# Attention on one core: where TensorE and VectorE load the bin numbers of a batch's tiles

## The reference, cut to what matters

```python
h = jnp.maximum(_layernorm(x, axis=-1), 0.0)
h = (h @ W.T).reshape(N, H, OUT)
a_src = (h * att_src).sum(-1)
a_dst = (h * att_dst).sum(-1)
alpha = jax.nn.leaky_relu(a_src[src] + a_dst[dst], 0.2)
amax = jax.ops.segment_max(alpha, dst, num_segments=N)
ex = jnp.exp(alpha - amax[dst])
denom = jax.ops.segment_sum(ex, dst, num_segments=N)
w = ex / denom[dst]
msg = h[src] * w[:, :, None]
out = jax.ops.segment_sum(msg, dst, num_segments=N)
x = x + out.reshape(N, H * OUT) + bias
```

## Time and profile before

| | |
|---|---|
| median of 3 runs | 5701.16 us |
| lowest and highest | 5682.81 and 5708.14 us |
| the profiled execution | 5682.86 us, of it span 5681.1 us |
| PE busy over the span | 90% |
| DVE | 69% |
| ACT | 52% |
| POOL | 68% |

### The profile page before, as it was taken

The page is one execution under the profiler, slowest core; times in us unless marked ns, Lnnn a source line. Parts: engine busy times, 40 slices in busy tenths (PEclk is TensorE's granted clock), DMA queues, the critical chain, the costliest instruction groups (busy, mean ns, idle before and its releaser), DMA issues.

```text
span 5681.1 us, 160364 instructions
## 1 busy us (share of the span) xinstructions
PE 5111.3 (90%) x34188; PEld 4074.0 (72%) x34189; DVE 3923.1 (69%) x14222; ACT 2971.1 (52%) x8485; POOL 3871.0 (68%) x3713
## 2 busy tenths in 40 slices
PE   4888888888888886999999999999997999999999
PEld 3777777777777774677666666666665888887788
DVE  6777877878778776555455555555455888888887
ACT  3566666666666653333333333332223777777776
POOL 4777777777777774677777777777776555555553
PEclk7889889889889987999999999999998999999999
DMA  4522222222222234999888988888886999999997
GB/s 109 165 54 54 54 54 54 54 54 54 54 54 54 54 105 139 278 275 270 262 263 258 266 262 260 262 264 259 262 257 186 224 221 222 222 221 217 217 222 193
DMA packets 860128, 995.58 MB, mean 175 GB/s; under 512 B 307993, under 2 KB 663225, under 8 KB 859776
## 3 DMA queue, kind: packets, MB, share of 16 engines
q1 hardware_dynamic: 662496, 610.19, 39.9%
q0 software_dynamic: 190592, 379.87, 24.6%
q10 hardware_dynamic: 6816, 3.38, 0.2%
HBM read 728.41 MB, written 264.62 MB: 175 GB/s over the span
## 4 chain that ended last, share of the span: by engine, by line
PE 59%; DMA 9%; issue 9%; DVE 9%; POOL 8%; DVEq 3%; ACT 3%; POOLq 0%; ACTq 0%; SPq 0%
PE bank L1703 12%; PE bank L1536 12%; PE bank L1626 8%; PE bank L1628 7%; PE bank L1693 7%; DMA xr<-arena 6%; POOL xr L547 5%; PE bank L1457 3%; POOL arena L499 2%; DVE arena L945 2%; DVEq L251 2%; DVE arena L1048 2%; PE bank L1616 1%; DMA arena<-xr 1%; DVE arena L1028 1%
## 5 line engine op out<-in xcount | busy, mean ns | idle before, releaser
L499 POOL DMA_INDIRECT arena<-h_tab,arena x1612 | 1557.1, 966 | 543.0 <-issue 420.7
L547 POOL DMA_INDIRECT xr<-arena x1612 | 1568.5, 973 | 511.7 <-issue 352.6
L1536 PE MATMUL bank<-arena 128*128 128x136 f32 x6448 | 1311.0, 332 | 78.3 <-DVE arena L1048 11.0
L719 ACT ACTIVATE arena<-bank 128x256 f32<-128x256 f32 x1612 | 591.3, 384 | 1389.6 <-PE bank L1628 932.0
L1626 PE MATMUL bank<-arena 128*128 128x256 f32 x3224 | 1023.4, 400 | 91.8 <-DVE arena L1244 45.1
L1536 PEld LDWEIGHTS bank<-arena 128*128 128x128 f32 x6448 | 980.9, 214 | 162.6 <-DVE arena L1048 67.0
L561 POOL DMA_INDIRECT arena<-p_tab,arena x428 | 671.3, 1569 | 622.3 <-DMA arena<-p_tab,arena 498.4
L626 ACT ACTIVATE arena<-bank 128x256 bf16<-128x256 bf16 x1612 | 614.7, 381 | 792.8 <-PE bank L1457 708.6
L1628 PE MATMUL bank<-arena 128*128 128x256 f32 x3224 | 971.3, 383 | 0.0
L1703 PE MATMUL bank<-arena 128*128 128x257 f32 x3424 | 901.5, 386 | 6.3 <-issue 2.6
L1048 DVE TENSOR_TENSOR arena<-arena,bank 128x272 f32 x1612 | 693.6, 430 | 212.7 <-PE bank L1536 186.0
(11 more groups left out here) (260 smaller groups left out, 6595.3 us busy)
## 6 DMA issues: line engine op xcount, KB each, us to landing
arena<-xr SPq DMA_DIRECT2D x428, 520.0 KB
arena<-q_tab SPq DMA_DIRECT2D x1612, 128.0 KB
arena<-in_edge_attr SPq DMA_DIRECT2D x61, 832.0 KB
arena<-rel_tab SPq DMA_DIRECT2D x124, 224.0 KB
arena<-h_tab,arena POOLq DMA_INDIRECT x1612
xr<-arena POOLq DMA_INDIRECT x1612
arena<-rel_tab SPq DMA_DIRECT2D x124, 192.0 KB
xr<-arena SPq DMA_DIRECT2D x26, 520.0 KB
```

Of the source, the lines that this page charges most:

```text
L499: pool.indirect_dma_start(G[:, q, t, :], None, h_tab, bass.IndirectOffsetOnAxis(ap=idx[:, q, t:t + 1], axis=0)).then_inc(sem(f"gath{q}"), 16)
L547: pool.indirect_dma_start(xr, bass.IndirectOffsetOnAxis(ap=pos[:, q, t:t + 1], axis=0), Rb[:, t, :], None).then_inc(sem(f"scat{m}"), 16)
L1536: last = pe.matmul(PSB[3 + t % 2][:, k * H * MW:(k + 1) * H * MW], OH[:, (t + 2 * q) % 4, k * P:(k + 1) * P], flat(msg[:, t, :, :]), start ...
```

## The change

TensorE and VectorE no longer load 26 bin numbers at the head of a batch. VectorE loads four at t=1, four at each of t=6, 10, 14, 18 and 22, ahead of that step's `add_up`, and two behind the last step. TensorE loads four at each of t=2, 6, 10, 14, 18 and 22, between that step's `turn` and `expand`, and two behind the last step. That makes 7 loads for each engine and batch, and the same 26 integers. In the last two batches TensorE has no load before and none after. The two batches of TensorE that stand ahead of the first one (0 and 1) keep their load of 26.

```diff
-        def bins(engine, b, count):
+        def bins(engine, b, first, count):
 
             return nc.values_load_multi_w_load_instructions(
-                bin_row[0:1, bass.ds(b * RB, count)], engines=[engine], min_val=0, max_val=NT - 1,
+                bin_row[0:1, bass.ds(b * RB + first, count)], engines=[engine], min_val=0, max_val=NT - 1,
...
-                a = flat(acc[:, bass.ds(regs[t], 2), :])
+                a = flat(acc[:, bass.ds(regs[t % 4], 2), :])
...
-                regs = bins(ENG.DVE, b, BT)
...
                     if t == 1:
+                        regs = bins(ENG.DVE, b, 0, 4)
                         dve.wait_ge(sem("r_step"), 4 * b + 4)
...
+                    if t >= 6 and t % 4 == 2:
+                        regs = bins(ENG.DVE, b, t - 2, min(4, BT - (t - 2)))
                     if t >= 2:
                         add_up(b, t - 2, regs)
...
+                regs = bins(ENG.DVE, b, BT - 2, 2)
                 add_up(b, BT - 2, regs)
                 add_up(b, BT - 1, regs)
...
             def batch(b, q, ahead2=True, ahead1=True, first=False, table=""):
-                if ahead2:
-                    regs = bins(ENG.PE, b + 2, BT)
...
                     if ahead2:
                         turn(b + 2, q, t)
+                        if t % 4 == 2:
+                            regs = bins(ENG.PE, b + 2, t - 2, min(4, BT - (t - 2)))
                         if t >= 2:
                             expand(b + 2, q, t - 2, regs)
...
                 if ahead2:
+                    regs = bins(ENG.PE, b + 2, BT - 2, 2)
                     expand(b + 2, q, BT - 2, regs)
                     expand(b + 2, q, BT - 1, regs)
```

More of the change, by code:

```diff
@@ L1458, in turn, with expand @@
                 last.then_inc(sem("ohT_ps"), 1)
-            def expand(b, q, t, regs, first=False):
+            def expand(b, q, t, regs, first=False, late=False):
                 pe.wait_ge(sem("ohT_ready"), b * BT + t + 1)
@@ L1467, in expand @@
                     last = pe.matmul(ab_ps[half][:, j, :, :].rearrange("p s c -> p (s c)"), ohT[:, (t + 2 * q) % 4, k * P:(k + 1) * P],
-                                     flat(aT3[:, bass.ds(regs[t] + k, 1), :, :]), start=(k == 0), stop=(k == 1))
+                                     flat(aT3[:, bass.ds(regs[t if first or late else t % 4] + k, 1), :, :]), start=(k == 0), stop=(k == 1))
                 last.then_inc(sem("expanded"), 1)
@@ L1498, in _ @@
             pe.wait_ge(sem("hx_used"), NCH)
-            regs = bins(ENG.PE, 0, BT)
+            regs = bins(ENG.PE, 0, 0, BT)
             for t in range(BT):
@@ L1509, in _ @@
             chain_carry(0)
-            regs = bins(ENG.PE, 1, BT)
+            regs = bins(ENG.PE, 1, 0, BT)
             for t in range(BT):
@@ L1513, in _ @@
                 if t >= 2:
-                    expand(1, 1, t - 2, regs)
-            expand(1, 1, BT - 2, regs)
-            expand(1, 1, BT - 1, regs)
+                    expand(1, 1, t - 2, regs, late=True)
+            expand(1, 1, BT - 2, regs, late=True)
+            expand(1, 1, BT - 1, regs, late=True)
             def batch(b, q, ahead2=True, ahead1=True, first=False, table=""):
-                if ahead2:
-                    regs = bins(ENG.PE, b + 2, BT)
                 pe.wait_ge(sem("g_ready"), b + 1)
```

## The result

The changed kernel takes 5719.78 us (median; 5707.93 to 5729.64), the kernel before 5701.75 beside it: a ratio of 1.0029, 95% interval 1.0022 to 1.0036. I had forecast 5695, that is 6 us less than before. The time lies in my range, but the sign is wrong: 18 us slower, some 24 us beside my sum of -6.

The account below looks back on a forecast made before the run. POOL's gather issuing was taken to bound the attention at 32.9 us a batch. Steady state -1, start -2 and tail -2.5 gave -5.5, said as -6 us; forecast median 5695 against 5701.16 before, range 5675 to 5724.

Parts of the forecast that it names:

- my sum of -6: Whole kernel: -1 in steady state, -2 at the start, -2.5 at the tail, -5.5 us in total, said as -6.
- POOL bounds the attention, at 32.9 us a batch: Attention's steady part: POOL is saturated by issuing gathers, 1.265 us a tile, so the period stays at 32.9 us.
- That margin: At L963, DVE's first step needing a batch's gathers: consumers tied to POOL with only some 0.3 us in 32.9.
- its term for POOL's waits: Attention's steady part: POOL's 2 us of real waits are all that can be gained; 1 us taken.
- The head's load goes, 2.0 us: Batch head: DVE's and PE's loads of 26 registers overlap, so 2.0 us a batch leave the consumers' path.
- Loads of four cost 0.27 to 0.44: Small loads in the attention's steps: 0.35 us taken for four registers, ends 0.27 to 0.44.
- PE's loads are hidden: PE's small loads in the attention's steps: 0 to 0.4 us a load, mostly beside DVE's at the same step.
- DVE's loads are exposed, 1.65 us a batch: DVE's steps: loads at t=6, 18, 22 and two thirds of t=10 exposed, 1.65 us; 3.0 if all seven are.
- The clock gives 0.4 us back: PE after each head: without the stand its half-clock stretch may go or move, worth 0 to 0.7 us a batch; 0.4 taken.
- L963's wait goes from 0.27 to about 1 us: DVE's first step needing a batch's gathers: consumers' own time changes by -0.75 us a batch, which goes into this wait.
- The ends: Attention's start and last two batches: -2 us (-3.5 to +2) at the start, -2.5 (-4 to +2) at the tail.
- the second: Attention rival: consumers fall behind POOL, DVE's loads all exposed, clock giving nothing; +0.7 us a batch, 5741; 11 in 100.

Follow-up runs that it names:

- e7: No loads in the batches (four registers loaded once, sums to wrong bins) and POOL's wait for the aggregations removed, against the kernel before: ratio 0.9970.
- e12: Changed kernel with PE loading 12 registers at t=2, ahead of L963, and none at t=6 and t=10: ratio 0.9994 to the kernel before.
- e13: Changed kernel with PE's loads of t=6 and t=10 each split into two loads of two: ratio 1.0136 to the kernel before.
- e1: Kernel before with only PE loading in fours, DVE keeping its load of 26 at the head: ratio 1.0084 to the kernel before.
- e2: Kernel before with only DVE loading in fours, PE keeping its load of 26 at the head: ratio 0.9985 to the kernel before.
- e8b: No loads in the batches, with PE repeating tile 4's aggregation nine times over where it waits for L963: ratio 0.9981 to the kernel before.
- e10: Changed kernel with PE doing tile 4's aggregation three times over where it waits for L963: ratio 1.0017 to the kernel before.
- e6: Kernel before with POOL's wait for the aggregations before odd tiles' gathers removed: ratio 0.9981 to the kernel before.
- e5: Changed kernel with POOL's wait for the aggregations before odd tiles' gathers removed: 5682.54 us where the kernel before has 5695.82, ratio 0.9981.
- e3: Both engines load twice a batch, 12 registers at t=1 (PE t=2) and 14 at t=14: 5703.45 us beside 5688.88, ratio 1.0031.

## Why the prediction was wrong, point by point

1. *POOL bounds the attention, at 32.9 us a batch.* Right. e7 shows 32.76 as its floor.
2. *"Which leaves 2 us of real waits in 52 batches. POOL is saturated."* The number was right, the reading was not, and here the prediction failed. I took a wait that shows no time for one that has room. At the thirteen gathers with the long stop the room was next to nothing (3.33 us from tile 9 in the batch shown, of which 3.28 are needed), and each 0.1 us later there is 0.1 us in every fourth batch. I looked for the margin on one side only, at L963, and wrote of its 0.3 us: "That margin decides this case." So my sum kept the period at 32.9 us where it came to 33.22, and its term for POOL's waits, -1 us of 2, stands against 17.5 us of holds. The earlier trace rows had the hint: 62.2 us before L499 were put down to PE's L1536, and 1344 - 349.8 / 0.305 leaves some 200 gathers whose last release was an aggregation.
3. *The head's load goes, 2.0 us.* Right: 6.3 us are left before L945 of 123.5.
4. *Loads of four cost 0.27 to 0.44.* Right: 0.335 on PE, 0.344 on DVE, and the address operation 0.051 to 0.057, put at 0.1. The one of two, though, which I had put at 0.2, takes 0.54; it stands at the batch's end, where e12 keeps it without a loss. My 0.082 us a register mixes two kinds of count, as the last section shows. The Trainium skill, "DMA: Bandwidth & Descriptors", section "Latency and other measured facts", has a floor of about 600 ns; 358 loads from on-chip memory with a median of 335 disagree.
5. *PE's loads are hidden.* Wrong, the second step that failed. I went by the earlier trace rows, from a stage in which PE's sequencer is far ahead of its engine. In the attention PE stood 42.7 us before L1470, and e12, e13, e1 show what it's worth: with the two loads moved from behind L963 (e12) the 18 us are gone, and with more of them there (e13) the loss grows to 1.0136. I had written that the attention's PE "is less far ahead of its engine", had put 0 to 0.4 us on a load, and then took it to lie beside DVE's. e2 shows the reverse: it is DVE's loads that show no price.
6. *DVE's loads are exposed, 1.65 us a batch.* They are on DVE (27.9 us before L1064), but with no price: e2 is faster than before by 9 us.
7. *The clock gives 0.4 us back.* Wrong in its sign. The half clock didn't become less (399 and 393 us of 1808); it moved from the steps behind the head, where it held POOL by next to nothing (2.4 us of holds in all), to those behind L963 (19 us before, 218 after). e8b shows what that costs in a kernel without loads, e10 that it's a part here. I had written "may go or move" and then priced only its going.
8. *L963's wait goes from 0.27 to about 1 us.* Right: 0.86, 44.9 us in 52 batches. It was bought with point 7, since this wait is what PE stands for. Own time of the consumers: with POOL free, period less L963's wait is 32.63 (e6) and 32.18 (e5), -0.45 us a batch where I had -0.75.
9. *The ends.* The tail gave -3.3 for -2.5. The start cost +1.9 where I took -2, within its bounds (-3.5 to +2).

The rivals: the second, in its milder form (+0.1 to +0.3 us a batch, 5705 to 5718), comes near the time, 0.34 us a batch, but by another way; its mark, gaps of POOL "in every batch", isn't there, and its mechanism, exposed loads on DVE, isn't either. No rival of mine had POOL waiting for the consumers.

What stays open: what POOL's sequencer does in the 3483 ns, and how the 18 us divide between loads and clock exactly, as each load also moves the stretches at half clock, and what share is DVE's late start at L963, which no run changed by itself. What e3 loses outside the tenth gather is open too. Of the 5.5 us of the first kind, e10 takes all and so does e12; of the 11.7 at the long stop, e12 takes 6.6 and e10 1.6. Why a stop of that length comes at the same gathers in kernels so different isn't settled either.

## What to carry to other kernels

If the engine that sets the pace also waits for its consumers, measure the room on both sides: a wait with no visible time may have none to give, and from then on every tenth of a microsecond between the two meeting points counts. Before moving small stops off an engine's head, ask what the steps in which they land are waited for by; here a stop of 2.1 us at the head was cheaper than two of 0.335 us behind L963. And time saved ahead of a wait only lengthens the wait: here PE came out of it at half its clock.

## What the runs showed of the hardware that I had not expected

Every 104th gather, POOL's sequencer stood 3483 ns behind L498, alike in before, after and the variant without loads; in the kernels without that wait no gather was late. A load of two registers takes longer than one of four: in the changed kernel the last load of each batch (51 in the stretch, on each engine) took 0.53 to 0.56 us, the other six 0.33 to 0.35, and e13's loads of two took 0.54 wherever they stood.

The counts fall into two rows. PE's loads of 4 and 12 took 0.335 and 0.85 us (e12), DVE's of 8 0.598 where nothing held it up; PE's of 2, 14 and 26 took 0.54, 1.33 and 2.10. Within each row that is about 0.065 us a register, and the second row lies some 0.34 us above the first. So 26 in one load was of the dearer kind. These are six counts, and no run tests the reason. e3's loads of 12 and 14:

```profile
L251 PEldq TENSOR_LOAD <-arena x103: 851/1329/1344, 307.7 to 1993.0; - x103
```

The profile's page counts 187 instruction-fetch packets on one queue for the kernel before and 51 for the changed one:

```profile
q14 instruction: 51, 0.42, 0.0%
```

I found no time that goes with them.
